# Attention stages of a two-layer transformer kernel: normalisation folded into the projection, values' scale and bias folded into the output weights, one Newton step from a logarithm, activation tables loaded at the start of a stage

## The reference

```python
def _layernorm(x, axis=-1, eps=1e-05):
    m = jnp.mean(x, axis=axis, keepdims=True)
    v = jnp.var(x, axis=axis, keepdims=True)
    return (x - m) / jnp.sqrt(v + eps)
...
        qkv = (x @ Wqkv.T).reshape(b, n, 3, H, dh)
...
        q = (x @ Wq + bq).reshape(b, s, NH, HD)
        k = (x @ Wk + bk).reshape(b, s, NH, HD)
        v = (x @ Wv + bv).reshape(b, s, NH, HD)
        q = _layernorm(q, q_scale, q_bias)
        k = _layernorm(k, k_scale, k_bias)
        v = _layernorm(v, v_scale, v_bias)
        scale = HD ** (-0.5)
        scores = jnp.einsum('bqhd,bkhd->bhqk', q, k) * scale
        probs = jax.nn.softmax(scores, axis=-1)
        out = jnp.einsum('bhqk,bkhd->bqhd', probs, v).reshape(b, s, NH * HD)
        return out @ Wo + bo
```

## Time and profile before

| | |
|---|---|
| timed runs, median (lowest to highest) | 1912.04 us (1908.57 to 1916.41) |
| profiled execution, its own time | 1891.98 us |
| span in the trace | 1890.2 us |
| TensorE busy | 1355.6 us (72%) |
| VectorE busy | 1184.6 us (63%) |
| GpSimd busy | 941.9 us (50%) |
| ScalarE busy | 718.7 us (38%) |
| mean granted TensorE clock | 0.811 |

### The profile page before, as it was taken

How to read it: one execution, slowest core, us unless ns; L and a number is a source line. 1 busy time by engine, 2 the same in 40 slices (tenths; PEclk the granted TensorE clock), 3 DMA queues, 4 the chain that set the end, 5 groups by cost and what they waited for, 6 DMA issues and landing times. The chain is left out here.

```text
span 1890.2 us, 34789 instructions
## 1 busy us (share of the span) xinstructions
PE 1355.6 (72%) x10592; PEld 873.5 (46%) x10592; DVE 1184.6 (63%) x4256; ACT 718.7 (38%) x1340; POOL 941.9 (50%) x1276
## 2 busy tenths in 40 slices
PE   2359929988889859963369916777777777876990
PEld 2249914444444428962258803333333333335880
DVE  6622256888888632228845547877787787745555
ACT  1112215666666512210023313544444544532330
POOL 5745534455555224547747745444544544433770
PEclk9999957999999959985579956866776676767995
DMA  9312217553000002222158710000000000004874
GB/s 292 97 51 72 68 45 155 114 119 70 22 20 13 13 17 63 72 79 77 58 150 243 226 56 12 7 18 14 16 15 13 17 6 7 13 18 144 238 231 141
DMA packets 105373, 146.40 MB, mean 77 GB/s; under 512 B 14192, under 2 KB 84336, under 8 KB 105264
## 3 DMA queue, kind: packets, MB, share of 16 engines
q1 hardware_dynamic: 85824, 107.13, 21.4%
q0 software_dynamic: 17408, 35.82, 5.6%
q10 hardware_dynamic: 2032, 2.10, 0.4%
HBM read 80.59 MB, written 64.40 MB: 77 GB/s over the span
## 5 line engine op out<-in xcount | busy, mean ns | idle before, releaser
L1370 ACT ACTIVATE a_PT<-a_psE 128x512 f32<-128x512 f32 (+1 forms) x512 | 276.0, 545 | 300.7 <-PE a_psE L1539 297.8
L1074 DVE TENSOR_REDUCE a_mx<-a_psS 128x2 f32<-128x512 f32 (+1 forms) x512 | 308.4, 615 | 18.9 <-PE a_psS L1502 17.7
L1502 PE MATMUL a_psS<-a_KT,a_QT 54*128 54x256 bf16 (+1 forms) x1024 | 203.9, 302 | 76.4 <-DVE a_mx L1074 62.5
L1539 PE MATMUL a_psE<-a_QM,a_KT 56*128 56x256 bf16 (+1 forms) x1024 | 208.6, 306 | 1.5 <-issue 0.8
L1563 PE MATMUL a_psV<-a_PT,a_vx 128*32 128x256 f32 (+1 forms) x2048 | 185.9, 442 | 0.0
L1975 POOL DMA_INDIRECT slots_y<-e_y,e_ids x160 | 155.7, 973 | 46.6 <-issue 24.4
L1897 PE MATMUL e_psH<-e_rowsT,e_w 128*128 128x256 f32 x640 | 160.3, 395 | 5.1 <-DMA e_w<-in_pack 3.7
L1502 PEld LDWEIGHTS a_psS<-a_KT,a_QT 54*128 54x128 bf16 x1024 | 61.6, 100 | 206.5 <-issue 108.1
L1811 POOL DMA_INDIRECT slots_y<-e_y,e_ids x128 | 124.6, 974 | 48.2 <-POOL e_ids L1809 28.7
L1775 ACT ACTIVATE e_hT<-e_psH 128x1024 f32<-128x1024 f32 x64 | 65.5, 1024 | 179.5 <-PE e_psH L1748 179.5
L1897 PEld LDWEIGHTS e_psH<-e_rowsT,e_w 128*128 128x128 f32 x640 | 118.5, 195 | 23.5 <-issue 5.1
(11 more groups left out here) (337 smaller groups left out, 3258.4 us busy)
## 6 DMA issues: line engine op xcount, KB each, us to landing
e_w<-in_pack SPq DMA_DIRECT2D x80, 450.0 KB
slots_x<-tail SPq DMA_DIRECT2D x8, 2193.0 KB, 13.5
e_rows<-slots_x SPq DMA_DIRECT2D x80, 129.0 KB, 2.9
e_rows<-spans_x SPq DMA_DIRECT2D x64, 129.0 KB
a_got<-slots_y SPq DMA_DIRECT2D x32, 256.0 KB, 2.7
t_got<-slots_y SPq DMA_DIRECT2D x32, 256.0 KB, 2.8
slots_y<-e_y,e_ids POOLq DMA_INDIRECT x288, 2.2
spans_x<-tail SPq DMA_DIRECT2D x4, 1032.0 KB, 17.1
```

What stands on the lines that cost most here:

```text
L1074: nc.vector.tensor_reduce(mx[u][:, t, 4 * g + r:4 * g + r + 3:2], psS[c % 2][:, :, 0:cols], AX, ALU.max).then_inc(s_max, 1)
L1370: nc.scalar.activation(PT[:, c % 4, :, q0:SEQ], psE[c % 2][:, :, q0:SEQ], ACT.Exp).then_inc(s_e, 1)
L1502: ins = nc.tensor.matmul(psS[c % 2][:, hh, 0:cols], QT[u][64 * r:64 * r + MAXR, k, t * P:(t + 1) * P], KT[u][64 * r:64 * r + MAXR, k, 0:co ...
L1539: ins = nc.tensor.matmul(psE[c % 2][:, hh, q0:SEQ], KT[u][64 * r:64 * r + MAXR + 2, k, kt * P:(kt + 1) * P], QM[64 * r:64 * r + MAXR + 2, ...
```

## The change

1. Layer normalisation of the projection's input. (x - mean) W equals x (W - column means of W), since the mean is over the 128 inputs. The column means are made once by TensorE (`mean_of`, a matrix of 1/128), and subtracted from `wqkv`. Per batch ScalarE copies x to `xs` (`tokens_out`), TensorE transposes and projects that, and `project_out` multiplies by the row's `rstd`. `norm.dve_apply` is not called any more.
2. Values. Their scale goes into the rows of the output weights; their bias times the output weights, plus bo, becomes `shift`, which a matmul with `mean_of` adds to the output in each batch. GpSimd writes the values times the head's factor (`scale_values`); VectorE's `values_out` and GpSimd's `output_bias` go, and `scale_heads` covers the 512 columns of queries and keys.
3. The factor 1/sqrt(variance). ScalarE takes the logarithm (`heads_log`) and one unit later the exponential of -0.5 of it; `refine` does one Newton step.
4. The tables of ScalarE's functions are loaded at the head of attention and expert stages.
5. In routing without capacity, three small VectorE operations per batch that nothing reads are left out.

```diff
@@ -480,7 +479,8 @@
                 self.R[:, :, :].rearrange("p k e -> p (k e)").unsqueeze(1).to_broadcast([P, TPB, TOPK * E]), ALU.add))
-            nc.vector.tensor_copy(self.M_all[:, bass.ds(b * TPB, TPB), :, :], m)
+            if self.capacity:
+                nc.vector.tensor_copy(self.M_all[:, bass.ds(b * TPB, TPB), :, :], m)
@@ -517,18 +517,12 @@
                                                keep.base[:, :].unsqueeze(1).to_broadcast([P, TPB, E]), ALU.add))
-            link.later(nc.vector.tensor_tensor(
-                self.prod[:, u, 0, :, :], m.rearrange("p t k e -> p (t k) e"),
-                self.A[:, u, :, :, :].rearrange("p t k e -> p (t k) e"), ALU.mult))
...
                 self.B[:, u, 1, :, :].unsqueeze(2).to_broadcast([P, TPB, TOPK, E]), ALU.mult))
-            nc.vector.tensor_reduce(
-                self.loc[:, bass.ds(b * TPB, TPB), :],
-                self.prod[:, u, 0, :, :].rearrange("p (t k) e -> p t k e", t=TPB), AX, ALU.add)
@@ -950,39 +954,42 @@
-            def refine(b):
+            def refine(b, u):
...
-                for n in range(3):
-                    chain(nc.gpsimd.tensor_tensor(hv[:, 4, :], hv[:, 3, :], hv[:, 3, :], ALU.mult))
-                    chain(nc.gpsimd.tensor_tensor(hv[:, 5, :], hv[:, 4, :], hv[:, 1, :], ALU.mult))
-                    chain(nc.gpsimd.tensor_scalar(hv[:, 6, :], hv[:, 5, :], -0.5, 1.5, ALU.mult, ALU.add))
-                    if n < 2:
-                        chain(nc.gpsimd.tensor_tensor(hv[:, 3, :], hv[:, 6, :], hv[:, 3, :], ALU.mult))
-                    else:
-                        nc.gpsimd.tensor_tensor(hv[:, 7, :], hv[:, 6, :], hv[:, 3, :], ALU.mult).then_inc(s_hn, 1)
+                wait(pool, s_v, b - 1)
+                chain(nc.gpsimd.tensor_tensor(hv[:, 4, :], hv[:, 3, :], hv[:, 3, :], ALU.mult))
+                chain(nc.gpsimd.tensor_tensor(hv[:, 5, :], hv[:, 4, :], hv[:, 1, :], ALU.mult))
+                chain(nc.gpsimd.tensor_scalar(hv[:, 4, :], hv[:, 5, :], -0.5, 1.5, ALU.mult, ALU.add))
+                nc.gpsimd.tensor_tensor(hv[:, 6 + u, :], hv[:, 4, :], hv[:, 3, :], ALU.mult).then_inc(s_hn, 1)
+
+            def head_scale(u):
+                return hv[:, 6 + u, :].rearrange("p (t h) -> p t h", t=TPB)
...
-                    pt2[:, :, :].rearrange("p t (h d) -> p (t h) d", d=DH),
-                    pr[:, u, :, :].rearrange("p t (h d) -> p (t h) d", d=DH),
-                    hv[:, 7, :].unsqueeze(2).to_broadcast([P, TPB * 3 * HEADS, DH]), ALU.mult))
+                    pt2[:, :, :].rearrange("p t (h d) -> p t h d", d=DH),
+                    pr[:, u, :, 0:2 * D].rearrange("p t (h d) -> p t h d", d=DH),
+                    head_scale(u)[:, :, 0:2 * HEADS].unsqueeze(3).to_broadcast([P, TPB, 2 * HEADS, DH]), ALU.mult))
...
-                    pt[:, u, :, :], pt2[:, :, :],
-                    par[:, SC0:SC0 + QKV].unsqueeze(1).to_broadcast([P, TPB, QKV]), ALU.mult))
+                    pt[:, u, :, 0:2 * D], pt2[:, :, :],
+                    par[:, SC0:SC0 + 2 * D].unsqueeze(1).to_broadcast([P, TPB, 2 * D]), ALU.mult))
...
-            def output_bias(b):
-
+            def scale_values(b, u):
+
+                wait(pool, s_V, UNITS * (b - 1))
+                pool.wait_ge(s_hn, b + 1)
...
-                    keep.x[:, bass.ds(b * TPB, TPB), :], keep.x[:, bass.ds(b * TPB, TPB), :],
-                    par[:, BO0:BO0 + D].unsqueeze(1).to_broadcast([P, TPB, D]), ALU.add).then_inc(s_xb, 1)
+                    vx[u][:, :, :, 0:DH], pr[:, u, :, 2 * D:QKV].rearrange("p t (h d) -> p t h d", d=DH),
+                    head_scale(u)[:, :, 2 * HEADS:3 * HEADS].unsqueeze(3).to_broadcast([P, TPB, HEADS, DH]),
+                    ALU.mult).then_inc(s_v, 1)
@@ -997,10 +1004,10 @@
                     scale_heads(s + 1, v)
+                if has(s) and not causal:
+                    scale_values(s, u)
                 if has(s + 1):
                     left_of_a(s + 1, v)
-                if has(s) and not causal:
-                    output_bias(s)
                 if has(s + 1):
@@ -1012,7 +1019,7 @@
                 if has(s + 2) and not causal:
-                    refine(s + 2)
+                    refine(s + 2, u)
                 chain.restart()
@@ -1031,27 +1038,18 @@
+                    dve.wait_ge(norm.s_rstd, b + 1)
...
-                nc.vector.tensor_tensor(pr[:, u, t, :], psA[:, 0:QKV], par[:, BI0:BI0 + QKV], ALU.add).then_inc(s_pr, 1)
+                nc.vector.scalar_tensor_tensor(
+                    out=pr[:, u, t, :], in0=psA[:, 0:QKV], scalar=norm.rstd[:, u, t:t + 1],
+                    in1=par[:, BI0:BI0 + QKV], op0=ALU.mult, op1=ALU.add).then_inc(s_pr, 1)
...
-                link(nc.vector.tensor_scalar(hv[:, 1, :], hv[:, 0, :], 1.0 / DH, QK_EPS, ALU.mult, ALU.add))
-
-                nc.vector.tensor_scalar(hv[:, 2, :], hv[:, 1, :].bitcast(I32), -0.5 * LN2 / 2 ** 23,
-                                        0.5 * LN2 * (127 - 0.043), ALU.mult, ALU.add).then_inc(s_hv, 1)
-
-            def values_out(b, u):
-
-                wait(dve, s_V, UNITS * (b - 1))
-                dve.wait_ge(s_qk, 2 * (b + 1))
-                nc.vector.tensor_tensor(
-                    vx[u][:, :, :, 0:DH], pt[:, u, :, 2 * D:QKV].rearrange("p t (h d) -> p t h d", d=DH),
-                    par[:, SB0 + 2 * D:SB0 + QKV].rearrange("p (h d) -> p h d", d=DH).unsqueeze(1)
-                    .to_broadcast([P, TPB, HEADS, DH]), ALU.add).then_inc(s_v, 1)
+                nc.vector.tensor_scalar(hv[:, 1, :], hv[:, 0, :], 1.0 / DH, QK_EPS, ALU.mult, ALU.add).then_inc(s_hv, 1)
@@ -1112,8 +1110,6 @@
-                if not causal:
-                    dve.wait_ge(s_xb, b + 1)
@@ -1145,8 +1141,6 @@
-                if has(s) and not causal:
-                    values_out(s, u)
@@ -1204,8 +1198,6 @@
-                if has(s + 3):
-                    norm.dve_apply(dve, s + 3, v)
@@ -1265,17 +1258,31 @@
-                    nc.vector.tensor_copy(wqkv[:, :], par[:, 0:QKV]).then_inc(s_ready, 1)
+                    dve.wait_ge(s_means, 1)
+                    nc.vector.tensor_tensor(wqkv[:, :], par[:, 0:QKV], psA[:, 0:QKV], ALU.subtract).then_inc(s_ready, 1)
...
+                    for n, col in enumerate((SC0, SB0)):
+                        link.later(nc.vector.tensor_tensor(picked[:, n, :], keep.ident[:, :],
+                                                           par[:, col + 2 * D:col + QKV], ALU.mult))
+                    link.sync()
+                    link(nc.vector.tensor_reduce(vcol[:, :], picked[:, :, :], AX, ALU.add))
+                    nc.vector.tensor_copy(vrep[:, :], vcol[:, 1:2].to_broadcast([P, P])).then_inc(s_mean_of, 1)
+                    dve.wait_ge(s_means, 1)
+                    link.later(nc.vector.tensor_tensor(wqkv[:, :], par[:, 0:QKV], psA[:, 0:QKV], ALU.subtract))
+                    dve.wait_ge(s_means, 2)
+                    for t in range(TPB):
+                        link.later(nc.vector.tensor_tensor(shift[:, t, :], psD[:, 0:D], par[:, BO0:BO0 + D], ALU.add))
+                    link.later(nc.vector.tensor_scalar(par[:, WO0:WO0 + D], par[:, WO0:WO0 + D], vcol[:, 0:1], None,
+                                                       ALU.mult))
+                    link.sync()
@@ -1300,6 +1307,11 @@
+            def tokens_out(b, u):
+                act.wait_ge(comb.s_added, b + 1)
+                wait(act, s_xaT_ps, b - 1)
+                nc.scalar.copy(xs[:, u, :, :], keep.x[:, bass.ds(b * TPB, TPB), :]).then_inc(s_xs, 1)
+
@@ -1307,9 +1319,11 @@
+                    act.wait_ge(norm.s_rstd, b + 1)
...
-                nc.scalar.copy(pr[:, u, t, :], psA[:, 0:QKV]).then_inc(s_pr, 1)
+                nc.scalar.activation(pr[:, u, t, :], psA[:, 0:QKV], ACT.Identity,
+                                     scale=norm.rstd[:, u, t:t + 1]).then_inc(s_pr, 1)
@@ -1327,9 +1341,13 @@
+            def heads_log(b):
+                act.wait_ge(s_hv, b + 1)
+                nc.scalar.activation(hv[:, 2, :], hv[:, 1, :], ACT.Ln).then_inc(s_ln, 1)
+
...
-                act.wait_ge(s_hv, b + 1)
-                nc.scalar.activation(hv[:, 3, :], hv[:, 2, :], ACT.Exp).then_inc(s_hr, 1)
+                act.wait_ge(s_ln, b + 1)
+                nc.scalar.activation(hv[:, 3, :], hv[:, 2, :], ACT.Exp, scale=-0.5).then_inc(s_hr, 1)
@@ -1397,6 +1415,8 @@
+                if has(s + 3):
+                    tokens_out(s + 3, v)
@@ -1410,8 +1430,10 @@
+                    heads_log(s + 2)
+                exps(13, 14)
+                if has(s + 2) and not causal:
...
-                exps(13, 14)
@@ -1420,16 +1442,23 @@
+            nc.scalar.preload_act_table_set("natural_log_exp_and_others")
...
+            pe.wait_ge(s_par, 16)
+            pe.wait_ge(s_mean_of, 1)
+            nc.tensor.matmul(psA[:, 0:QKV], mean_of[:, :], par[:, 0:QKV], start=True, stop=True).then_inc(s_means, 1)
+            if not causal:
+                pe.wait_ge(s_mean_of, 2)
```

(12 more changed lines are left out.)

## The result

The changed kernel has a median of 1810.15 us (1809.08 to 1816.7, 4 runs) beside 1910.3 us for the kernel before on the same chip; the ratio is 0.9557, interval 0.9438 to 0.9676. The profiled execution took 1816.7 us (span 1814.8) and the one before 1891.98: 75.2 less.

A forecast was written before the change was run, and what follows sets the result against it. Bound: the second attention, VectorE waiting behind GpSimd's port lock, TensorE idling, then slowed at clock 0.70. Terms -36 + 10 - 6 - 12 - 6 - 6 - 3 - 1 = -60 took 1912 to 1852 us; range 1832 to 1878, 80% range 1812 to 1892.

The forecast's parts named there:

- rival 1: Second attention reaches full clock, a batch takes 28.4 us: 94 us faster in all, 1818 us; chance 15%.
- End of batch, -36: Second attention: projection input leaves VectorE, GpSimd ends earlier, TensorE waits less: 41 us gained, 5 lost behind the maxima.
- Clock, -12: Second attention: less idle time lets some batches keep 2.4 GHz, 1 us per batch, 12 us faster.
- Output product, +10: Second attention: the added 256-column matmul costs 0.8 us per batch, nothing hides it; 10 us slower, range 5 to 16.
- First attention, -6: First attention: half the projection input's cost lies before the routed rows TensorE waits for; 13 batches, 6 us faster.
- rival 3: First attention loses its full clock, up to 7 us more per batch, 91 us slower, 1943 us; chance 6%.
- VectorE's small work, -6: Second attention: value copy, exponent trick and three routing operations go; 0.5 us per batch, 6 us faster.
- fill and setup, -6: Fills and setup: fewer refinement operations and no first normalised input, against added setup work; together 6 us faster.
- token stage, -3: Token stage: VectorE loses three operations of about 180 ns per batch, half overlapping; 3 us faster.
- Tables, -1: ScalarE's table loads move to stage fronts; those in expert loops are hidden, only fills count: 1 us faster.
- Rival 2: The port wait only moves to other VectorE instructions; the input is worth only 11 us, 1889 us; chance 15%.
- theory 2: From the follow-ups: the number of VectorE and GpSimd operations counts, anywhere in the batch; logarithm 15 to 35 us faster.

The follow-up runs named there:

- the second measurement: The changed kernel unchanged, run again on another chip against the kernel before: 1815.83 us, ratio 0.9624.
- the chain alone: Kernel before with only the rsqrt's start value from ScalarE's logarithm, one Newton step instead of three, table loaded early: 1863.99 us, ratio 0.9775.
- the input alone: Kernel before with only the projection run on unnormalised tokens and scaled by the reciprocal deviation on leaving PSUM: 1884.66 us, ratio 0.9898.
- the new order of GpSimd: Changed kernel, second attention: third long GpSimd product waits for VectorE's routed rows, values' product moved behind the first split product: 1821.71 us, ratio 0.9633.
- The filler in the kernel before: Kernel before plus 16 unused matmuls per batch in TensorE's wait for the routed rows, second attention only: 1890.27 us, ratio 0.9974.
- the values alone: Kernel before with only the values' scale in the output weights, biases by one matmul per batch, values scaled on GpSimd: 1886.11 us, ratio 0.9897.
- the new order with matmuls: Changed kernel with GpSimd's products reordered and unused matmuls in TensorE's wait, 4 per batch in first attention, 6 in second: 1788.35 us, ratio 0.946.

## Why the prediction was right, and where it was not

The forecast was 60 us off the time before, 44 of them in the second attention's loop; measured were 75.2 between the profiled executions and 70.7 in that loop. By the ratio 0.9557 the 1912 us become 1827 (1840 by the second measurement's 0.9624). So the forecast of 1852 had the direction, the stage and the place right and was too small: 1827 lies outside its own range of 1832 to 1878, nearer to rival 1's 1818, and inside the 80% range only because that takes rival 1 in. Point by point:

- *End of batch, -36.* The place was right, and the joint size nearly: TensorE's wait there fell by 30.8 us (65.7 to 34.9), where 41 less 5 was forecast; the routed rows are at 544 ns, not 420. What the step had wrong is whose gain it is. It began with "the projection input is gone from VectorE" and took the shorter GpSimd chain as what makes the rest whole. The runs show the reverse: the chain alone gives 2.3%, the input alone 1.0% (these intervals overlap, but the batches, 2.96 and 0.94 us shorter, are further apart than two profiles of one kernel). The 5 us for the instructions behind the maxima did not come (407 ns beside 433). The reason stands in the traces: the second of them, which reads two tiles, waits for GpSimd as the copies do. It takes 0.30 us with GpSimd idle, and otherwise what GpSimd's operation has left and some 0.15 more. Below are the kernel before with GpSimd idle; the GpSimd operation beside the 0.72 us at 418.58 in the earlier trace rows; and the first batch of the second attention with the new order of GpSimd, both engines:

```profile
325.23 0.30 DVE L1081 SCALAR_TENSOR_TENSOR a_ext<-a_mx,a_ext 128x32 bf16<-128x32 f32 x1
418.38 0.73 POOL L946 TENSOR_TENSOR a_pt<-a_pr,a_cosn 128x256 f32<-128x256 f32 x1
1155.80 1.18 DVE L1080 SCALAR_TENSOR_TENSOR a_ext<-a_mx,a_ext 128x32 bf16<-128x32 f32 x1
1155.74 1.07 POOL L973 TENSOR_TENSOR a_pt<-a_pr,a_hv 128x512 f32<-128x512 f32 x1
```

  So the mechanism was right and the neighbour was not: in the middle batches one of GpSimd's small operations still lies there (0.08 to 0.34 us left), and only in the first does a wide one. (A slip without weight: 10.2 less 6.0 less 0.7 is 3.5 us, not 3.3.)
- *Clock, -12.* The term that was mis-sized. The same matmuls take 39 us less in twelve batches. The filler in the kernel before suggests why it was kept: there 33 us of such gain left 16.5 in the window, with VectorE's maxima next; the changed kernel's VectorE is 41.4 us shorter (322.10 to 280.71). That this is the reason is argued, not shown.
- *Output product, +10.* Busy 15.5 us, worth nothing: leaving it out changed neither batch nor time. VectorE's wait for it rose from 19.6 us (9.6 and 10.0, in two groups) to 26.2, 0.4 per batch where 0.8 was forecast; against the same kernel without the product it is 0.8 to 1.1. The step that failed is "nothing hides that": that wait is not what sets the batch.
- *First attention, -6.* Right for an undisturbed batch, 23.8 to 23.4 us, 13 times 0.4. But its clock went from 1.00 to 0.95 and single batches gave it back: 1.2 us were left in one profile, 7.7 in the other. Its sign for rival 3, a clock under 1.00 there, came, with a size far below 91 us. The argument against it ("its idle time gets shorter, not longer") did not protect: idle before the routed rows fell from 1.75 to 1.38 us per batch there, and the clock fell all the same. But it is not shown that the change is the cause: the values alone, which leave this stage as it was, had it at 0.92 with batches up to 29.5 us. What recurs with the fold, in all its profiles but that of the new order with matmuls, are single batches 1 to 1.5 us longer than their neighbours.
- *VectorE's small work, -6; fill and setup, -6; token stage, -3.* The latter two gave 2.9 and 1.4 us. The first is inside the loop's sum and was not measured apart.
- *Tables, -1.* Right for the experts. It missed that the change needs its table set: without it 24 us are lost (its interval and that of the changed kernel touch; the loads and the 21.7 us in the loop do not leave it open). That is a condition of the logarithm, not an edit beside it.
- *Rival 1* (full clock, 1818 us) is nearer to 1827 than the forecast, without its mechanism: the clock is 0.79, the batch 30.64, not 28.4. *Rival 2* does not hold for the whole change, but for its first part, and for the new order of GpSimd.

What stays open: the three single parts add to 4.3%, about the whole, but the intervals are as wide as a part; whether theory 2's count of operations has a share; and why single batches of the first attention lose clock.

## What to carry to other kernels

When two engines keep each other out, look for what delays the one that comes first, not only for what the waiting one does: eight small operations of 0.3 to 0.4 us on GpSimd, with no other engine waiting for them directly, decided where 4 us of long products fell. An operation taken off the waiting engine at such a place only passes the wait to the next copy, and holding a long product back does the same. Where TensorE's clock is low in a stage with short waits, try a few matmuls without use in the wait: here they gave 33 us in the changed kernel with GpSimd's new order, and nothing that could be measured in the kernel before, where VectorE was next.

## What the runs showed of the hardware

- A copy of four columns on VectorE takes 0.16 us, or as long as GpSimd's product has left: 0.91, 0.92 us; over a batch loop 868 or 1047 ns in the mean.
- A VectorE instruction with two inputs waits in the same way: the one behind the maxima takes 0.30 us alone, 0.72 with 0.53 us left of a GpSimd operation, 1.18 with 1.01 left. Its mean is 303 to 442 ns in the twelve batches of the second attention of these kernels, where mostly a small GpSimd operation lies beside it, and 618 in the first attention of the kernel before, where a wider one does. The row maxima, read from PSUM, take 0.68 us with 1.21 us of a GpSimd product left, as without.
- A table load takes 1.28 us, and ScalarE's next activation starts right behind it.
- Six matmuls of 512 columns in each batch's wait, 16.2 us in all for twelve batches, go with a clock of 0.89 in the changed kernel's first order (0.79 and 0.82 in its two profiles without them, on other chips), and with 0.82 in the other order (0.76 without them, on the same chip).
